# A two-layer conditioned block on one core: the first loads and the down weight's quantisation take other places in layer 0's opening steps

## The chip, the cores and the metric

The kernel runs on one NeuronCore of a Trainium2 chip. The metric is the device time of one launch in microseconds (us), as the median of several runs; a lower time is better. The trace shown below is one profiled execution of the same program. Engine names: PE is TensorE (matmuls; PEld its weight loads), DVE is VectorE, ACT is ScalarE, POOL is GpSimd, SP is SyncE, which here only issues transfers. "SPq" and "ACTq" are instructions that issue a transfer (DMA) from that engine's queue.

## What is computed

Eight sequences of 512 tokens with model width 256 go through two layers, both steered by a vector `cond` per sequence. Layer 0 is a gated feed-forward with a quantised second matmul; layer 1 is adaptive-norm attention with 16 heads, then adaptive-norm SwiGLU. Layer 0, where the change lies, is:

```python
scale = cond @ norm_w.T + 1.0
h = x * (scale[:, None, :] * rsqrt(mean(x * x, -1) + EPS))
val, gate = split(h @ up_w.T, 2, axis=-1)              # up_w: 2048 x 256
h = val * gelu(gate)
s = 127 / clip(max|h| over a row);  hq = clip(round(h * s), -128, 127) / s
t = 1 / clip(mean|down_w|);         wq = clip(round(down_w * t), -1, 1) / t
x1 = hq @ wq.T + x                                     # down_w: 256 x 1024
```

## The kernel before, in words

Layer 0 runs as 32 tiles of 128 tokens. Every engine has its own instruction queue, written out by `phase1_program`: for each step n it first puts what `before_<engine>(n)` gives, then the tile's work `<engine>_tile(n)`. An engine works its queue strictly in this order, and a semaphore wait in it holds all that stands behind. Step n loads and scales tile n, does the up matmuls, the gate and the quantisation of tile n-1 (`UP = 1`), and the down matmul of tile n-3 (`DOWN = 3`). In what follows, m is the number of a tile.

One step, by engine. SP loads `xk` (the tile transposed) and `xt` (its tokens in rows), and issues the transposing transfer `qT <- h_q`. ACT makes `xs` = scaled `xk` (needs `par`, the layer's scale vector), the sum of squares of `xt`, and two gelu halves. DVE copies `xs` to its rounded part (`x_high`, line 412), makes `ms` (415), multiplies gate half 0 (`gate(0)`, 422), then gate half 1 (`gate(1)`), takes the row maximum (452), scales (462) and ends with `h_q` (474). POOL makes the remainder part of `xs` (348, signals `x_split`) and the powers. PE does 12 matmuls of 512 columns for half 0 (gate bank, value bank), then the down matmul of tile n-3 (393), then 12 more for half 1. The matmuls in fp32r are done in three products of high and low parts, so a weight needs its high part (an ACT copy) and its low part (a DVE subtraction).

Weights in the opening. `load_up_sp` (step 1 of SP) loads the up weight in four pieces of 512 columns (512 KB each). `up_high_act` (step 1 of ACT, line 510) makes a piece's high part, `up_low_dve` (step 1 of DVE, line 633) its low part; PE's tile 0 waits for `up_low` piece by piece. `load_small_act` (step 0 of ACT) issues four transfers: `cond`, the layer-0 scale vector's weight (64 KB), the other six vectors' weights (384 KB) and `out_b`. The last two are needed from step 4 of PE and step 5 of DVE on.

The down weight (1 MB) is loaded by SP in step 2 (`load_down_sp`). DVE sums its absolute values in step 1, between `gate(0)` and `gate(1)` (`down_sum_dve`, line 638). In step 2, PE sums that over partitions (`mean_pe`, after its first 12 matmuls); DVE, again between `gate(0)` and `gate(1)`, makes the mean and its reciprocal (`down_mean_dve`), and then three passes over 128 x 2048 elements (`down_quantised_dve`, lines 653, 656, 659), the last of which brings the semaphore `down_steps` to 6. PE's first down matmul, in step 3 between its two groups of 12, waits for it:

```python
if live(n, DOWN):
    m = n - DOWN
    pe.wait_ge(q_turned[m % 2], (m // 2 + 1) * 16)
    if m == 0:
        pe.wait_ge(down_steps, 6)
```

After layer 0, layer 1's attention of one sequence and the feed-forward of the sequence before run together.

Of the kernel before, what the change touches and what calls it, by code (L numbers as in the profile page):

```python
# [5 lines left out]
def cond_seq_kernel(nc, x_tok, xT, condT, vec_wT, up_wT, down_wT, wqT, wkT, wvT, woT, gate_wT, hidden_wT,  # L6
# [40 lines left out]
    with ctx:  # L47
# [359 lines left out]
        def dve_tile(dve, n):  # L407
            if live(n, 0):
                dve.wait_ge(x_scaled, credited(x_scaled, n + 1))
                if n >= 2:  # L410
                    dve.wait_ge(up_val_done, 2 * n - 2)
                nc.vector.tensor_copy(xs_part[0][:, n % 2, :, :], xs[:]).then_inc(x_high, 1)
                dve.wait_ge(square_done, n + 1)
                dve.wait_ge(rstd_done, credited(rstd_done, n))
                nc.vector.tensor_scalar(ms[:], ss[:], 1.0 / D, EPS, ALU.mult, ALU.add).then_inc(ms_done, 1)  # L415

            def gate(j):

                m = n - UP
                dve.wait_ge(up_val_done, 2 * m + j + 1)  # L420
                dve.wait_ge(gelu_done, credited(gelu_done, 2 * m + j + 1))
                nc.vector.scalar_tensor_tensor(h[:, j * W:(j + 1) * W], val_bank[j][:],  # L422
                                               rstd[:, m % 2:m % 2 + 1], gelu[:, j, :], ALU.mult, ALU.mult) \
                    .then_inc(h_done, 1)
            if live(n, UP):
                gate(0)
            if n == 1:
                down_sum_dve(dve)
            if n == 2:
                down_mean_dve(dve)  # L430
                down_quantised_dve(dve)
            if live(n, DOWN):
                m = n - DOWN
                nc.vector.tensor_tensor(dequant[:, m % 2:m % 2 + 1], clipped[:, m % 4:m % 4 + 1], wdeq[:], ALU.mult) \
                    .then_inc(dequant_done, 1)
                dve.wait_ge(dequant_done, m + 1)
                dve.wait_ge(down_done, credited(down_done, m + 1))
                if m >= T:
                    dve.wait_ge(x1_stored[m % T], credited(x1_stored[m % T], m // T * 16))
                nc.vector.scalar_tensor_tensor(x1t[:, m % T, :], down_bank[:, 0:D], dequant[:, m % 2:m % 2 + 1],  # L440
                                               xt[:, m % (T + 1), :], ALU.mult, ALU.add).then_inc(x1_done, 1)
            if live(n, NORM):
                m = n - NORM
                dve.wait_ge(square2_done, m + 1)
                dve.wait_ge(rstd2_done, credited(rstd2_done, m))
                nc.vector.tensor_scalar(ms2[:], ss2[:], 1.0 / D, EPS, ALU.mult, ALU.add).then_inc(ms2_done, 1)
            if live(n, UP):
                m = n - UP
                gate(1)

                dve.wait_ge(h_done, credited(h_done, 2 * m + 2))
                nc.vector.tensor_reduce(amax[:, 0:1], h[:], AX.X, ALU.max, apply_absolute_value=True) \  # L452
                    .then_inc(scale_steps, 1)
                dve.wait_ge(scale_steps, 4 * m + 1)
                nc.vector.tensor_scalar(clipped[:, m % 4:m % 4 + 1], amax[:, 0:1], 1e-5, None, ALU.max) \
                    .then_inc(scale_steps, 1)
                dve.wait_ge(scale_steps, 4 * m + 2)
                nc.vector.reciprocal(amax[:, 1:2], clipped[:, m % 4:m % 4 + 1]).then_inc(scale_steps, 1)
                dve.wait_ge(scale_steps, 4 * m + 3)
                nc.vector.tensor_scalar(amax[:, 2:3], amax[:, 1:2], QMAX, None, ALU.mult).then_inc(scale_steps, 1)  # L460
                dve.wait_ge(scale_steps, 4 * m + 4)
                nc.vector.tensor_scalar(h_rounded[:], h[:], amax[:, 2:3], ROUND, ALU.mult, ALU.add) \
                    .then_inc(rounded, 1)
            if live(n, NORM):
                m = n - NORM
                dve.wait_ge(rstd2_done, credited(rstd2_done, m + 1))
                dve.wait_ge(xn_transposed, credited(xn_transposed, m))
                nc.vector.tensor_scalar(xn[:], x1t[:, m % T, :], rstd2[:], None, ALU.mult).then_inc(xn_done, 1)
            if live(n, UP):
                m = n - UP  # L470
                dve.wait_ge(rounded, m + 1)
                if m >= 2:
                    dve.wait_ge(q_turned[m % 2], m // 2 * 16)
                nc.vector.tensor_scalar(h_q[:, m % 2, :], h_rounded[:], ROUND, QMAX, ALU.subtract, ALU.min) \
                    .then_inc(quantised, 1)

        def load_up_sp(sp):
            src = up_wT.rearrange("(k p) n -> p k n", p=P)
            for i, cols in enumerate(CHUNKS):
                sp.dma_start(up_st[:, :, cols], src[:, :, cols]).then_inc(up_loaded[i], 16)  # L480

        def load_down_sp(sp):
# [19 lines left out]
        def load_small_act(act):  # L502
            act.dma_start(cond_sb[:], condT).then_inc(scale_loaded, 16)
            act.dma_start(vec_w[:, 0, :], vec_wT[:, 0, :]).then_inc(scale_loaded, 16)
            act.dma_start(vec_w[:, 1:7, :], vec_wT[:, 1:7, :]).then_inc(small_loaded, 16)
            act.dma_start(outb_sb[:], out_b.partition_broadcast(B)).then_inc(small_loaded, 16)

# [128 lines left out]
        def down_sum_dve(dve):  # L636
            dve.wait_ge(down_loaded, 16)
            nc.vector.tensor_reduce(absum[:], down_st[:], AX.XY, ALU.add, apply_absolute_value=True) \
                .then_inc(down_steps, 1)
# [7 lines left out]
            nc.vector.reciprocal(wscale[:], mean[:]).then_inc(down_steps, 1)  # L647
            dve.wait_ge(wdeq_ready, 1)

        def down_quantised_dve(dve):  # L650

            dve.wait_ge(down_steps, 3)
            nc.vector.tensor_scalar(down_st[:], down_st[:], wscale[:], 1.0, ALU.mult, ALU.min) \
                .then_inc(down_steps, 1)
            dve.wait_ge(down_steps, 4)
            nc.vector.tensor_scalar(down_st[:], down_st[:], -1.0, ROUND, ALU.max, ALU.add) \
                .then_inc(down_steps, 1)
            dve.wait_ge(down_steps, 5)
            nc.vector.tensor_scalar(down_q[:], down_st[:], ROUND, None, ALU.subtract).then_inc(down_steps, 1)

# [11 lines left out]
        def pieces_at(n):  # L672

            return [i for i in range(len(PIECES)) if n == (3 + i if i < 2 else 5 + (i - 2) // 2)]
# [15 lines left out]
        STACK_SP = [(0, half, r) for half in range(2) for r in range(ROWS // HD)] + [(1, half, 0) for half in range(2)]  # L690

        def before_sp(sp, n):
            if n == 1:
                load_up_sp(sp)
            elif n == 2:
                load_down_sp(sp)
                load_late_sp(sp, (0, 1, 2, 3))
            elif n == 3:
                sp.wait_ge(up_low, len(CHUNKS))
                load_late_sp(sp, (4, 5))  # L700
            elif n == T + 2:
                sp.wait_ge(down_steps, 6)
                load_late_sp(sp, (6,))
            elif n == 2 * T:
                store_alphas_sp(sp)
            elif n == XA_AT:
                for s in range(2):
                    sp.wait_ge(xa_stored[s], credited(xa_stored[s], 2 * 16))
                load_xa_sp(sp, 0)
            elif n == XA_NEXT_AT:  # L710
                for s in range(2):
                    sp.wait_ge(xa_stored[s], credited(xa_stored[s], 4 * 16))
                sp.wait_ge(q_in_low, credited(q_in_low, 1))
                load_xa_sp(sp, 1)
            elif 0 <= n - STACK_AT < 4:
                sp.wait_ge(stack_ones, 2)
                for w, half, r in STACK_SP[2 * (n - STACK_AT):2 * (n - STACK_AT) + 2]:
                    sp.wait_ge(pair_free[w], credited(pair_free[w], 1))
                    stack_dma(sp, 0, w, half, r)

        def before_act(act, n):
            if n == 0:
                load_small_act(act)
            elif n == 1:
                for i in range(len(CHUNKS)):
                    up_high_act(act, i)
            for i in pieces_at(n):
                late_high_act(act, i)
            if n == SPLIT_AT:
# [51 lines left out]
        def before_dve(dve, n):  # L781
            if n == 0:
                scale_dve(dve)
            elif n == 1:
                for i in range(len(CHUNKS)):
                    up_low_dve(dve, i)
            elif n == STORE:
                vectors_dve(dve)
                alphas_dve(dve)
# [1083 lines left out]
```

## Time and profile before

| | us |
|---|---|
| median of 3 runs (lowest, highest) | 996.54 (996.38, 996.85) |
| the profiled execution's own time | 994.97 |
| span of its instructions | 993.1 |
| PE busy in the span | 965.3 (97%) |
| DVE, ACT, POOL busy | 727.9, 552.2, 271.6 |

All times of rows are counted from the first instruction. A row of the timeline is one instruction, or several alike in a run; in brackets stands how long the engine had been idle before it and what ended that. PE's matmuls are pipelined, so the durations of single ones overlap and a "busy" PE includes its overlap. DMA shares are of the 16 DMA engines of the core, and can exceed 1 a little where packets overlap.

### The profile page before, as it was taken

How to read it: one execution, taken by the hardware profiler on the slowest of the kernel's cores; microseconds unless marked ns; L12 is line 12 of the kernel's file. 1: busy time of each engine (PE TensorE's matmuls, PEld its weight loads, DVE VectorE, ACT ScalarE, POOL GpSimd, SP SyncE). 2: the span in 40 equal slices, each digit the busy share in tenths (PEclk: the TensorE clock that was granted, in tenths of full speed). 3: DMA queues.
4: the chain of work that ended last, by engine and by line, in shares of the span. 5: the costliest groups of instructions: out<-in, count | busy, mean ns of one | idle time of the engine just before them, and what ended most of it. 6: DMA issues, size and time to landing. Idle time of an engine off the chain costs nothing.

```text
span 993.1 us, 15671 instructions
## 1 busy us (share of the span) xinstructions
PE 965.3 (97%) x5411; PEld 603.8 (61%) x5411; DVE 727.9 (73%) x1216; ACT 552.2 (56%) x1160; POOL 271.6 (27%) x260
## 2 busy tenths in 40 slices
PE   5999999999999999999999999999999999999998
PEld 4777777776534555655664565556556655655577
DVE  5888888999577777678777767876776777677343
ACT  5466554554655656466556646554764665466632
POOL 1265422221101132222213222231222133134142
PEclk9999999999999999999999999999999999999999
DMA  9645556343431122133021302301230213020000
GB/s 285 150 121 126 139 129 160 96 120 78 107 91 30 65 80 45 41 100 70 1 87 55 70 13 96 90 15 67 73 71 4 84 44 60 30 90 7 2 27 22
DMA packets 93742, 75.45 MB, mean 76 GB/s; under 512 B 44880, under 2 KB 79768, under 8 KB 93664
## 3 DMA queue, kind: packets, MB, share of 16 engines
q1 hardware_dynamic: 81344, 61.36, 22.8%
q10 hardware_dynamic: 12320, 13.09, 5.4%
q8 instruction: 44, 0.72, 0.3%
q14 instruction: 34, 0.28, 0.1%
HBM read 27.73 MB, written 12.61 MB: 41 GB/s over the span
## 4 chain that ended last, share of the span: by engine, by line
PE 86%; DVE 7%; issue 2%; ACT 2%; DMA 2%; ACTq 1%; SPq 0%; POOL 0%; DVEq 0%; POOLq 0%
PE bank L1247 20%; PE bank L370 13%; PE bank L1002 12%; PE bank L1021 12%; PE bank L1291 9%; PE raw_pair L926 5%; PE bank L851 4%; PE bank L902 2%; PE bank L1084 2%; DVE amax L452 2%; PE bank L393 2%; DVE h L422 1%; PE bank L401 1%; PE bank L1397 1%; DVE rowmax L958 1%
## 5 line engine op out<-in xcount | busy, mean ns | idle before, releaser
L1010 ACT ACTIVATE probs<-bank 128x512 f32<-128x512 f32 x512 | 277.0, 598 | 172.1 <-PE bank L1002 165.9
L958 DVE TENSOR_REDUCE rowmax<-raw_pair 128x2 f32<-128x1024 f32 x224 | 273.7, 1222 | 114.8 <-PE raw_pair L926 114.8
L370 PE MATMUL bank<-up_w,xs_part 128*128 128x512 f32 x768 | 191.9, 403 | 5.4 <-issue 3.6
L1002 PE MATMUL bank<-q_stack,k_stack 50*128 50x512 f32 x512 | 189.4, 449 | 2.3 <-ACT probs L1010 1.7
L370 PEld LDWEIGHTS bank<-up_w,xs_part 128*128 128x128 f32 x768 | 142.2, 190 | 39.9 <-issue 6.6
L926 PE MATMUL raw_pair<-k_stack,q_stack 48*128 48x512 f32 x448 | 157.7, 449 | 0.4 <-DVE rowmax L958 0.3
L1277 POOL TENSOR_TENSOR hid<-scratch,hid 128x512 fp32r<-128x512 f32 x64 | 82.4, 1288 | 195.4 <-ACT hid L1273 195.4
L1021 PE MATMUL bank<-probs,v_ext 128*17 128x512 f32 x1024 | 134.8, 598 | 0.9 <-issue 0.9
L1002 PEld LDWEIGHTS bank<-q_stack,k_stack 50*128 50x128 f32 x512 | 76.9, 185 | 84.0 <-issue 51.1
L1291 PEld LDWEIGHTS bank<-out_w,hid 128*128 128x128 f32 x672 | 81.4, 188 | 30.0 <-issue 30.0
L1291 PE MATMUL bank<-out_w,hid 128*128 128x256 f32 x672 | 92.0, 287 | 0.0
L300 ACT ACTIVATE gelu<-bank,rstd 128x512 f32<-128x512 f32 x64 | 44.0, 688 | 57.4 <-PE bank L370 57.4
L1255 ACT ACTIVATE scratch<-bank 128x512 f32<-128x512 f32 x64 | 38.0, 594 | 59.4 <-PE bank L1247 56.6
L926 PEld LDWEIGHTS raw_pair<-k_stack,q_stack 48*128 48x128 f32 x448 | 63.1, 185 | 6.1 <-issue 4.0
L422 DVE SCALAR_TENSOR_TENSOR h<-bank,rstd,gelu 128x512 f32<-128x512 f32 x64 | 47.7, 746 | 23.2 <-PE bank L370 23.2
L348 POOL TENSOR_TENSOR xs_part<-xs,xs_part 128x256 fp32r<-128x256 f32 x32 | 23.6, 738 | 145.5 <-DVE ms L415 127.0
L1259 DVE SCALAR_TENSOR_TENSOR scratch<-scratch,bank 128x512 f32<-128x512 f32 x64 | 43.4, 678 | 14.3 <-ACT scratch L1255 14.3
L1247 PEld LDWEIGHTS bank<-xf_part,gate_w 128*128 128x128 f32 x192 | 33.6, 188 | 33.0 <-issue 27.2
L1247 PE MATMUL bank<-xf_part,hidden_w 128*128 128x512 f32 x192 | 53.2, 412 | 0.0
L1247 PE MATMUL bank<-xf_part,gate_w 128*128 128x512 f32 x192 | 53.1, 412 | 0.0
L1266 DVE SCALAR_TENSOR_TENSOR scratch<-scratch,bank 128x512 f32<-128x512 f32 x64 | 43.9, 686 | 10.2 <-POOL hid L1277 7.7
L1247 PE MATMUL bank<-xa_part,gate_w 128*128 128x512 f32 x186 | 50.4, 406 | 0.0
(185 smaller groups left out, 1332.3 us busy)
## 6 DMA issues: line engine op xcount, KB each, us to landing
q_stack<-split SPq DMA_DIRECT2D x54, 128.0 KB, 3.0
q_stack<-hid SPq DMA_DIRECT2D x42, 128.0 KB, 2.9
k_stack<-hid SPq DMA_DIRECT2D x42, 128.0 KB, 2.9
xk<-xT SPq DMA_DIRECT2D x32, 128.0 KB, 2.8
xt<-x_tok SPq DMA_DIRECT2D x32, 128.0 KB, 2.6
x_spill<-x1t ACTq DMA_DIRECT2D x32, 128.0 KB, 2.5
xa_spill<-xa ACTq DMA_DIRECT2D x32, 128.0 KB, 2.3
x_in<-xa_spill SPq DMA_DIRECT2D x8, 512.0 KB, 5.2
```

What stands on the lines that cost most here:

```text
L300: nc.scalar.activation(gelu[:, j, :], gate_bank[j][:], ACT.Gelu, scale=rstd[:, m % 2:m % 2 + 1]) \
L370: last = nc.tensor.matmul(bank[j][:], xs_part[a][:, m % 2, k, :], up_w[w][:, k, col + j * W:col + (j + 1) * W], start=(i == 0), stop=(i == ...
L422: nc.vector.scalar_tensor_tensor(h[:, j * W:(j + 1) * W], val_bank[j][:], rstd[:, m % 2:m % 2 + 1], gelu[:, j, :], ALU.mult, ALU.mult) \
L926: mm = nc.tensor.matmul(raw_pair[:, half, :], q_stack[rows, slot, qt * P:(qt + 1) * P], k_stack[rows, slot, :], start=True, stop=True)
L958: nc.vector.reduce_max(rowmax[:, e:e + RAWS + 1:RAWS], raw_pair[:], AX.X).then_inc(raw_read, 1)
L1002: nc.tensor.matmul(score_bank[c % 3][:], k_stack[rows, slot, kt * P:(kt + 1) * P], q_stack[rows, slot, :], start=True, stop=True).then_inc ...
L1010: nc.scalar.activation(probs[:, (kt % 2) * J + j, :], score_bank[c % 3][:], ACT.Exp).then_inc(exp_done, 1)
L1021: last = nc.tensor.matmul(o_bank[32 * j:32 * j + HD + 1, :], v_ext[:, kt, J * g + j, :], probs[:, (kt % 2) * J + j, :], start=(kt == 0), s ...
L1247: last = nc.tensor.matmul(work_bank(n, f, spare)[:], weight[wp][:, k, f * P:(f + 1) * P], xf_of(c)[a][:, k, :], start=(i == 0), stop=(i == 5))
L1266: nc.vector.scalar_tensor_tensor(scratch[1][:], scratch[0][:], 0.5, work_bank(1, f, spare)[:], ALU.mult, ALU.mult) \
L1277: nc.gpsimd.tensor_tensor(hid[1][:, f, :], scratch[1][:], hid[0][:, f, :].bitcast(f32), ALU.subtract) \
L1291: last = nc.tensor.matmul(ab[m][:, (t % HALF) * D:(t % HALF + 1) * D], hid[a][:, f, t * P:(t + 1) * P], out_w[wp][:, f, :], start=(i == 0) ...
```

## The change

The first 512 KB piece of the up weight is loaded by SP in step 0, ahead of `xk` and `xt` of tile 0; the other three stay in step 1. ACT makes that piece's high part in step 0, behind its small loads and ahead of tile 0's scaling. The six other vectors' weights and `out_b` are no longer issued in ACT's step 0 but behind the other three high parts in its step 1. DVE's sum of the down weight moves from between the two gates of step 1 to the place behind the four low parts, ahead of tile 1's `x_high`. The three quantising passes are split: the first stays where all three were, the second goes behind `gate(1)`, the third behind `h_q`, all in step 2.

```diff
@@ dve_tile @@
             if live(n, UP):
                 gate(0)
-            if n == 1:
-                down_sum_dve(dve)
             if n == 2:
                 down_mean_dve(dve)
-                down_quantised_dve(dve)
+                down_scaled_dve(dve)
...
                 gate(1)
+                if n == 2:
+                    down_rounded_dve(dve)
...
                 nc.vector.tensor_scalar(h_q[:, m % 2, :], h_rounded[:], ROUND, QMAX, ALU.subtract, ALU.min) \
                     .then_inc(quantised, 1)
+            if n == 2:
+                down_quantised_dve(dve)
@@ loads @@
-        def load_up_sp(sp):
+        def load_up_sp(sp, pieces):
             src = up_wT.rearrange("(k p) n -> p k n", p=P)
-            for i, cols in enumerate(CHUNKS):
+            for i in pieces:
+                cols = CHUNKS[i]
                 sp.dma_start(up_st[:, :, cols], src[:, :, cols]).then_inc(up_loaded[i], 16)
...
             act.dma_start(vec_w[:, 0, :], vec_wT[:, 0, :]).then_inc(scale_loaded, 16)
+
+        def load_vectors_act(act):
             act.dma_start(vec_w[:, 1:7, :], vec_wT[:, 1:7, :]).then_inc(small_loaded, 16)
             act.dma_start(outb_sb[:], out_b.partition_broadcast(B)).then_inc(small_loaded, 16)
@@ down_quantised_dve is cut in three, before each of its waits @@
-        def down_quantised_dve(dve):
+        def down_scaled_dve(dve):
             dve.wait_ge(down_steps, 3)
             nc.vector.tensor_scalar(down_st[:], down_st[:], wscale[:], 1.0, ALU.mult, ALU.min) \
                 .then_inc(down_steps, 1)
+
+        def down_rounded_dve(dve):
             dve.wait_ge(down_steps, 4)
             nc.vector.tensor_scalar(down_st[:], down_st[:], -1.0, ROUND, ALU.max, ALU.add) \
                 .then_inc(down_steps, 1)
+
+        def down_quantised_dve(dve):
             dve.wait_ge(down_steps, 5)
             nc.vector.tensor_scalar(down_q[:], down_st[:], ROUND, None, ALU.subtract).then_inc(down_steps, 1)
@@ before_sp @@
-            if n == 1:
-                load_up_sp(sp)
+            if n == 0:
+                load_up_sp(sp, (0,))
+            elif n == 1:
+                load_up_sp(sp, (1, 2, 3))
@@ before_act @@
             if n == 0:
                 load_small_act(act)
+                up_high_act(act, 0)
             elif n == 1:
-                for i in range(len(CHUNKS)):
+                for i in range(1, len(CHUNKS)):
                     up_high_act(act, i)
+                load_vectors_act(act)
@@ before_dve @@
             elif n == 1:
                 for i in range(len(CHUNKS)):
                     up_low_dve(dve, i)
+                down_sum_dve(dve)
```

## Rows read from the trace of the kernel before

**Rows 1.** Page, part 1: busy us (share of the span) xinstructions, by engine.
```profile
PE 965.3 (97%) x5411; PEld 603.8 (61%) x5411; DVE 727.9 (73%) x1216; ACT 552.2 (56%) x1160; POOL 271.6 (27%) x260
```

**Rows 2.** Timeline of PE (start us, us, what) in layer 0.
```profile
10.47 7.61 PE L370 MATMUL bank<-up_w,xs_part 128*128 128x512 f32 x24 [3.65 <-issue]
18.45 3.06 PE L370 MATMUL bank<-up_w,xs_part 128*128 128x512 f32 x12 [0.37 <-POOL xs_part L348]
...
25.86 3.06 PE L370 MATMUL bank<-up_w,xs_part 128*128 128x512 f32 x12 [1.33 <-POOL xs_part L348]
30.01 1.03 PE L393 MATMUL bank<-down_q,qT 128*128 128x256 bf16 x8 [1.09 <-issue]
...
54.89 5.82 PE L370 MATMUL bank<-up_w,xs_part 128*128 128x512 f32 x24
```

**Rows 3.** Timeline of DVE, steps 0 to 2: low part, sum, passes, first `h_q`.
```profile
9.14 1.23 DVE L633 TENSOR_TENSOR up_w<-up_st,up_w 128x1024 fp32r<-128x1024 f32 x1 [0.79 <-ACT up_w L510]
...
18.46 2.28 DVE L638 TENSOR_REDUCE absum<-down_st 128x1 f32<-128x2048 f32 x1
20.65 0.74 DVE L422 SCALAR_TENSOR_TENSOR h<-bank,rstd,gelu 128x512 f32<-128x512 f32 x1
...
24.04 0.69 DVE L474 TENSOR_SCALAR h_q<-h_rounded 128x1024 bf16<-128x1024 f32 x1
24.65 0.28 DVE L412 CAST xs_part<-xs 128x256 fp32r<-128x256 f32 x1
24.85 0.15 DVE L415 TENSOR_SCALAR ms<-ss 128x1 f32<-128x1 f32 x1
...
28.68 1.23 DVE L659 TENSOR_SCALAR down_q<-down_st 128x2048 bf16<-128x2048 f32 x1
...
33.23 0.69 DVE L474 TENSOR_SCALAR h_q<-h_rounded 128x1024 bf16<-128x1024 f32 x1
```

**Rows 4.** Timeline of ACT and ACTq, steps 0 to 2.
```profile
2.64 0.74 ACTq L506 DMA_DIRECT2D outb_sb<-out_b  x1
...
7.07 0.69 ACT L317 ACTIVATE xs<-xk,par 128x128 f32<-128x128 f32 x2 [2.29 <-DVE par L613]
8.07 1.04 ACT L510 ACTIVATE up_w<-up_st 128x1024 fp32r<-128x1024 f32 x1
...
14.70 1.28 ACT L300 ACT_TABLE_LOAD   x1
...
22.36 0.70 ACT L317 ACTIVATE xs<-xk,par 128x128 f32<-128x128 f32 x2 [1.51 <-DMA xk<-xT]
23.27 0.19 ACT L322 ACTIVATION_READ_ACCUMULATOR square_junk<-xt 128x1 f32 x1
```

**Rows 5.** Windows: us, busy us by engine, clock, DMA share, GB/s.
```profile
3.00:6.00 3.00, 0.00 (x0) 0.00 (x0) 1.00 0.87 226
6.00:9.00 3.00, 0.00 (x0) 0.00 (x0) 1.00 1.01 211
9.00:12.00 3.00, 1.53 (x4) 1.27 (x5) 1.00 1.03 367
```

**Rows 6.** DMA issues: KB, us from issue to landing (issued 1.66, 6.04, 17.11, 24.76).
```profile
up_st<-up_wT SPq DMA_DIRECT2D x1, 512.0 KB, 6.3
down_st<-down_wT SPq DMA_DIRECT2D x1, 1024.0 KB, 11.3
xk<-xT SPq DMA_DIRECT2D x1, 128.0 KB, 5.2
qT<-h_q SPq DMA_TRANSPOSE x1, 4.2
```

**Rows 7.** Timeline of PE at layer 0's end, and the granted clock of two windows there.
```profile
248.40 0.44 PE L401 MATMUL bank<-ident,xn 128*128 128x128 f32 x2 [2.31 <-DVE xn L468]
...
248.40:249.60 1.20, 0.98 (x4) 0.86 (x5) 1.00 0.00 0
249.60:253.00 3.40, 3.40 (x9) 2.30 (x7) 0.50 0.71 156
```

## The prediction

> **What bounds the kernel now.** I read four views in this order. The page's busy times say that PE works 97% of the span [rows 1], so a change counts only by the time at which PE gets through its queue. The timeline of PE shows where it stands still in the opening: it starts at 10.47, waits 0.37 at 18.45, 1.33 at 25.86 and 1.09 at 30.01 [rows 2]; from then on it is as good as gapless (24 matmuls in 5.82 in the steady step [rows 2]) until layer 0's end. So what the change is worth is one number: by how much PE's first down matmul, now at 30.01, moves, since all that follows on PE hangs on it at a fixed distance. The timeline of DVE says what it waits for: the third pass over the down weight runs 28.68 to 29.91, PE starts 0.10 later [rows 2, 3]; the transposed `qT` had landed at 24.76 + 4.2 = 28.96 [rows 6] and was not last. ACT's timeline and the DMA answers say what feeds DVE.
>
> **Start of PE.** Tile 0's `xs` starts at 7.07, when `par` comes [rows 4]. Piece 0 of the up weight lands at 1.66 + 6.3 = 7.96 now [rows 6]. Issued first and without 384 KB on the other queue it lands much earlier: 512 KB at 226 to 367 GB/s [rows 5] takes 1.4 to 2.3, and `xk` of 128 KB in front of it cannot delay it any more, so I estimate 4.5 to 6. Its high part (1.04 [rows 4]) is then hidden under the wait for `par`, up to a landing at 6.0; beyond that each us costs one. `xk` moved behind it is covered the same way. DVE is free for the low part at 9.14 - 0.79 = 8.35 [rows 3] and no longer waits: 8.4 to 9.6, PE at 9.7, 0.8 earlier. At the start PE runs slowly (24 matmuls in 7.61 against 5.82 [rows 2]), and most of the early start falls in that slow time, so tile 0's 24 end at about 17.5 instead of 18.1. The gain for the end is decided elsewhere.
>
> **Transfers.** The non-vector loads ran at 226 and 211 GB/s from 3 to 9 and at 367 after [rows 5]. These 6 us moved 1.31 MB, which takes 3.6 at 367; without the vectors' 0.39 MB as well, 2.5. So loads issued before the vectors can come 0 to 3.5 earlier; I take 2.8, since both the bytes and what slows them go. The down weight then lands not at 6.04 + 11.3 = 17.3 [rows 6] but at 14.5. The vectors now come behind the fourth high part, which ended at 14.70 [rows 4] and will end at about 12; their two issues (0.74 for one [rows 4], 1.4 for both) and the table load (1.28 [rows 4]) stand ahead of gelu half 0 and tile 1's `xs`, which is done by about 16, a us before DVE can take it. Their bytes hit the down weight's end: 0 to 1.1 (0.39 MB at 367), I take 0.2. Landing 14.7.
>
> The Trainium skill ("DMA: Bandwidth & Descriptors", section "Issuing engines are not separate DMA queues") says that transfers of ACT and SP run on the same 16 engines and interleave. A DMA share of 1.01 at only 211 GB/s [rows 5] fits that; by the rule alone moving bytes back returns nothing to loads behind them, tile 2's `xk` would stay at 22.3, and the shift worked out below would be 0.7 more.
>
> **The sum, moved ahead of tile 1 on DVE.** The low parts end at about 13.4 (8.4 + 4 x 1.23 [rows 3]). Before, the sum found its data there; now DVE waits for the landing, 14.7, and sums until 17.0 (2.28 [rows 3]). Queued behind this new wait are tile 1's `x_high`, so POOL's split and PE's tile 1, and both gates. From `x_high` to PE's start it is 25.86 - 24.65 = 1.21 [rows 2, 3], so PE starts tile 1 at 18.2 (18.45 before): nearly nothing. What is gained is on DVE: `gate(1)` of tile 0 comes at about 18.0 instead of 20.65, and, as far behind it as now (24.65 - 20.65 = 4.0 [rows 3]), tile 2's `x_high` could run at 22.0.
>
> **Step 2 of DVE.** `x_high` needs `xs` of tile 2, and that needs `xk`, which landed at 17.11 + 5.2 = 22.3, with ACT waiting for it [rows 4, 6]. By then all vector bytes have been moved in both kernels; only the slow rate can have been saved. 0 to 1.5 earlier, I take 0.7: `xs` from 21.65, and `ms` of tile 2 as far behind it as the read of the squares allows: 23.27 + 0.19 - 22.36 = 1.1 [rows 4], so 22.8. From `ms` at 24.85 to the end of the last instruction of the step, 33.23 + 0.69 = 33.92 [rows 3], are 9.07 us in which DVE does not rest. The change reorders these instructions and removes none. Before, the third pass stood ahead of `gate(1)`, the maximum and `h_q`; now it is last, behind them. So `down_steps` 6 comes at 22.8 + 9.1 = 31.9 and PE's down matmul at 32.0, against 30.01: **2.0 later**. Bounds: with the down weight at 13.9 and `xk` at 20.5, `ms` at 21.2, down matmul at 30.4, +0.4; with the down weight at 15.6 and `xk` unchanged, `ms` at 23.5, 32.7, +2.7. The first pass stays, the second pushes `h_q` of tile 1 by nothing that anyone waits for: its transposed form is needed a step later.
>
> **PE while it waits.** Tile 2's first half can start at max(22.4 + 1.2, 18.2 + 6.1) = 24.3 and ends at 27.35 (3.06 [rows 2]). PE then stands still until 32.0, 4.65 us. The one long pause in the trace outside the start is 2.31 us at 248.40, and behind it the granted clock fell to 0.50 from 249.60 to 253.00, the lower of the two levels, with PE busy throughout [rows 7]; before the pauses of 1.33 and 1.09 nothing fell. The nearest price: the slow start, 7.61 - 5.82 = 1.8, of which about 0.2 was a wait [rows 2]; so **1.6**. From both sides: 0.9 if part of the slow stretch lies in the pause, 2.9 if PE has to work longer before the clock returns. I take 1.6, as 3.4 us at half speed lose 1.7. After it, nothing gives the time back: `x_high` and `gate(0)` of tile 3 stand ready on DVE, and PE is gapless.
>
> **Sum**: +2.0 + 1.6 = +3.6. On the profiled execution's own 994.97 that is 998.6; the median of the runs is 1.57 above that execution, so **1000.1**.
>
> **Rivals.** (a) *The clock holds* through the pause: +2.0, 998.5. For it: a pause of 2.31 let 1.2 us of fast work pass before the fall [rows 7], so the fall depends on how pause and work lie. Against: the pause is twice as long. (b) *Loads early, clock falls*: +0.4 + 1.6 = +2.0, 998.5. (c) *Not slower*: `xk` of tile 2 and the down weight land so early that DVE's step 2 is set by DVE alone. The point from which it decides is `ms` of tile 2 at 20.8 (20.8 + 9.1 = 29.9, today's end of the third pass). That wants `xk` by 19.7, 2.6 earlier than now, and `gate(1)` of tile 0 at 17.0, when tile 0's matmuls have just ended. At its nearest bound, +0.4, with a clock that holds: 996.9; at 20.8: 996.5. (d) *Loads late*: the vectors' bytes sit on the down weight, +2.7 + 1.6 = +4.3, 1000.8, with a long slow clock 1002.1. (e) *The third pass isn't last for PE*: if `qT` took its place, 28.96 is earlier than any of these, so this changes nothing and gets no chance.
>
> **How the numbers follow.** Forecast 0.42; (a) 0.20; (b) 0.10; (c) 0.08; (d) 0.13; a path that I don't see 0.07. A measurement of this kernel can tell about 0.2% (2.0 us) from no change, so the bound is 998.5, on which (a) and (b) lie: half of each counts as slower. Slower: 0.40 + 0.10 + 0.05 + 0.13, less a little for my misreading of an engine's order, 0.65. Faster has no case of its own but the unseen path: 0.05. The rest, 0.30, is within 0.2%. The range goes from (c), 996.6, to the late loads with a longer slow clock, 1001.9.
>
> **What would show it.** Right: PE's start near 9.7; DVE idle ahead of L638, which starts at 14 to 15.5; `ms` of tile 2 at 21.2 to 23.5; the third pass as the last DVE instruction of step 2, near 31.9; an idle time of over 3 us ahead of the first L393 on PE, and a second stretch with the clock at 0.50 behind it. Wrong: a down matmul before 30.0, or a wait ahead of it that ends on `qT`. The forecast is wrong if the low parts or the gate instructions on DVE start much earlier than the landings allow here, or if PE finds other idle time later that swallows the shift.

## The result and the profile after

The changed kernel is slower: 998.28 us as the median of 20 runs (996.34 to 1003.15) against 995.46 of the kernel before in 20 runs beside it (993.66 to 996.85); the ratio is 1.0031, 95% interval 1.0022 to 1.0040. The profiled execution took 998.17 with a span of 996.4. The forecast was +3.6 us, ratio 1.0036; measured are 2.8 by the medians and 3.1 by the ratio.

PE's timeline of the changed kernel, from the start to the steady step; the columns are start us, us, and in brackets the idle time before:

```profile
10.18 11.17 PE L370 MATMUL bank<-up_w,xs_part 128*128 128x512 f32 x36 [3.26 <-issue]
21.18 0.28 PE L611 MATMUL bank<-absum,ones 128*128 128x1 f32 x2
21.32 5.83 PE L370 MATMUL bank<-up_w,xs_part 128*128 128x512 f32 x24
31.45 1.86 PE L393 MATMUL bank<-down_q,qT 128*128 128x256 bf16 x8 [4.31 <-issue]
32.97 4.42 PE L370 MATMUL bank<-up_w,xs_part 128*128 128x512 f32 x12
37.32 1.95 PE L584 MATMUL raw_pair<-cond_sb,vec_w 64*128 64x8 f32 x16
```

Against [rows 2], the waits of 0.37 and 1.33 are gone: tiles 0, 1 and the first half of tile 2 follow each other without a gap, and PE stands in front of its first down matmul at 27.15 instead of 28.92. There it waits 4.31 instead of 1.09, and starts 1.44 later than before. Behind that wait everything is slow: 8 down matmuls take 1.86 instead of 1.03 and the 12 up matmuls behind them 4.42 instead of 3.02 (the row that starts at 30.80 before), 2.2 us together. The windows of the same kernel say why (us, busy us of PE, PEld, DVE, ACT, POOL, then the granted clock, DMA share, GB/s):

```profile
27.15:29.20 2.05, 0.00 (x0) 0.00 (x0) 1.91 (x5) 1.20 (x4) 0.00 (x0) 0.99 0.62 172
29.20:31.40 2.20, 0.00 (x0) 0.00 (x0) 2.17 (x4) 0.00 (x0) 0.00 (x0) 0.50 0.00 0
31.40:36.00 4.60, 4.54 (x15) 3.53 (x16) 1.52 (x5) 0.08 (x1) 2.48 (x3) 0.50 0.54 118
```

The clock fell to its lower level in the middle of the pause and was still there for the next 4.6 us of PE's work, to 36.0. What PE waited for is the last row of DVE's step 2, which ends at 31.35, 0.10 before PE starts; `qT` had landed at 22.60 + 5.6 = 28.2. DVE's timeline of the changed kernel, where it answers to [rows 3]:

```profile
8.36 1.72 DVE L638 TENSOR_TENSOR up_w<-up_st,up_w 128x1024 fp32r<-128x1024 f32 x1
...
14.92 2.29 DVE L643 TENSOR_REDUCE absum<-down_st 128x1 f32<-128x2048 f32 x1 [1.45 <-DMA down_st<-down_wT]
...
22.48 0.28 DVE L412 CAST xs_part<-xs 128x256 fp32r<-128x256 f32 x1
22.69 0.14 DVE L415 TENSOR_SCALAR ms<-ss 128x1 f32<-128x1 f32 x1
...
23.92 1.28 DVE L658 TENSOR_SCALAR down_st<-down_st,wscale 128x2048 f32<-128x2048 f32 x1
25.13 0.74 DVE L422 SCALAR_TENSOR_TENSOR h<-bank,rstd,gelu 128x512 f32<-128x512 f32 x1
25.79 1.21 DVE L663 TENSOR_SCALAR down_st<-down_st 128x2048 f32<-128x2048 f32 x1
26.92 1.21 DVE L452 TENSOR_REDUCE amax<-h 128x1 f32<-128x1024 f32 x1
...
29.52 0.69 DVE L474 TENSOR_SCALAR h_q<-h_rounded 128x1024 bf16<-128x1024 f32 x1
30.13 1.22 DVE L668 TENSOR_SCALAR down_q<-down_st 128x2048 bf16<-128x2048 f32 x1
```

DVE's step 2 starts 2.2 us earlier than before (`ms` at 22.69 against 24.85), yet the third pass ends 1.44 later, at 31.35, because it is now the last instruction of the step. The loads did what was wanted: ACT's high part of piece 0 starts at 4.98 against 8.07 [rows 4], the down weight is there at 14.92 against 17.3 [rows 6], tile 2's `xk` at 21.5 against 22.3. ACT's timeline of the changed kernel:

```profile
4.98 1.06 ACT L515 ACTIVATE up_w<-up_st 128x1024 fp32r<-128x1024 f32 x1 [1.70 <-DMA up_st<-up_wT]
...
11.16 1.06 ACT L515 ACTIVATE up_w<-up_st 128x1024 fp32r<-128x1024 f32 x1 [0.34 <-DMA up_st<-up_wT]
...
21.53 0.70 ACT L317 ACTIVATE xs<-xk,par 128x128 f32<-128x128 f32 x2 [0.86 <-DMA xk<-xT]
```

### The profile page after: what moved, and what is told of

The parts are those of the page before. It is cut to its first block, busy times and chain, and to the rows that moved or that the text cites. A ratio compares the mean times of both kernels' runs of the same rounds, so it can differ in the third digit from the quotient of the medians.

```text
span 996.4 us, 15671 instructions
## 1 busy us (share of the span) xinstructions
PE 966.0 (97%) x5411; PEld 604.5 (61%) x5411; DVE 727.7 (73%) x1216; ACT 552.9 (55%) x1160; POOL 274.0 (28%) x260
## 3 DMA queue, kind: packets, MB, share of 16 engines
q1 hardware_dynamic: 81344, 61.36, 22.8%
## 4 chain that ended last, share of the span: by engine, by line
PE 86%; DVE 7%; issue 2%; DMA 2%; ACT 2%; ACTq 1%; POOL 0%; DVEq 0%; POOLq 0%
PE bank L1261 20%; PE bank L370 14%; PE bank L1016 12%; PE bank L1035 12%; PE bank L1305 9%; PE raw_pair L940 5%; PE bank L865 4%; PE bank L916 2%; PE bank L1098 2%; DVE amax L452 2%; PE bank L393 2%; DVE h L422 1%; PE bank L1411 1%; DVE rowmax L972 1%; PE bank L401 1%
## 5 line engine op out<-in xcount | busy, mean ns | idle before, releaser
L1077 POOL TENSOR_TENSOR split<-o_sb,split 128x512 fp32r<-128x512 f32 x15 | 19.3, 1287 | 113.7 <-ACT split L1073 113.7
```

## The experiments

Theory: the third pass's place makes PE's first down matmul late, and the long pause takes the clock down; the loads gain. Rivals: the loads' order or DVE's new wait ahead of the sum (1.45 us in the row above) costs; the clock plays no part. Each ratio is to the kernel before, run beside it on the same chip, with its 95% interval.

### One part undone: the passes back between the gates

```diff
                 down_scaled_dve(dve)
+                down_rounded_dve(dve)
+                down_quantised_dve(dve)
...
                 gate(1)
-                if n == 2:
-                    down_rounded_dve(dve)
...
-            if n == 2:
-                down_quantised_dve(dve)
```

> The changed kernel with one part undone: all three passes over the down weight stand again between the gates of step 2; the loads and the sum keep their new places. Theory (the third pass's place costs the time, directly and by the clock): the passes end near 27.7, the transposed qT lands at about 28.2 as in the changed kernel (issued 22.60, 5.6 to landing) and is now the last to come, the first L393 starts near 28.3 instead of 31.45 or 30.01, the wait ahead of it is 1 to 1.3, no slow clock follows; 1.7 us faster than before, ratio 0.998 to 0.9985. Rival (the wait of DVE for the down weight ahead of the sum, 1.45 us in the changed kernel, is what costs): that wait is still there, so this stays slower than before, ratio 1.001 or more.

Measured: ratio 0.9978 (0.9969 to 0.9987), faster than before. PE's timeline of this variant around the down matmul:

```profile
29.98 1.05 PE L393 MATMUL bank<-down_q,qT 128*128 128x256 bf16 x8 [1.67 <-DMA qT<-h_q]
30.79 3.03 PE L370 MATMUL bank<-up_w,xs_part 128*128 128x512 f32 x12
33.75 1.95 PE L582 MATMUL raw_pair<-cond_sb,vec_w 64*128 64x8 f32 x16
35.63 1.03 PE L601 MATMUL raw_pair<-vec_w,cond_sb 64*8 64x256 f32 x4
36.59 4.60 PE L370 MATMUL bank<-up_w,xs_part 128*128 128x512 f32 x12
```

The down matmul now waits for `qT`, as expected, and the rival falls: DVE's wait for the down weight is still in this variant. In this execution `qT` took 7.0 us to land (issued 22.95) and the matmul came at 29.98, later than the 28.3 expected. `qT` isn't the whole miss: tile 2's `xk` came late too, `xs` started at 23.31 (21.53 in the changed kernel, with the same loads), and the third pass ended at 29.51 where 27.7 was expected. The profiled execution was also the slowest of this variant's ten runs, 996.36 against a median of 993.43, so its rows show the order of the waits but not the usual times. One row speaks against a part of the theory: the matmuls at 36.59 took 4.60 instead of the 3.04 of the same row before, so the clock fell although the pause had been short. That is taken up below.

### One part alone: the passes in three places

The kernel before with the passes split as in the change, loads and sum untouched.

> The kernel before with one part of the change alone: the three passes in three places, loads and sum as before. Theory: the third pass becomes the last of a DVE step that ended at 33.92, so the first L393 starts at 34.0, 4.0 later than before; the wait ahead of it is about 5 us and the clock falls to its lower level behind it, another 1.6 to 2.3: +5.6 to +6.3 us, ratio 1.0056 to 1.0063. Rival (the load order and the sum cost the time): this is as fast as before, ratio within 0.001 of 1.

Measured: ratio 1.0047 (1.0034 to 1.0061), the slowest of all. The first L393 starts at 34.06 after a pause of 4.70, with the slow clock behind it (1.87 for the 8 matmuls, 4.24 for the 12 behind them). In the traces both shares are as expected: 4.05 for the place and 0.84 + 1.22 = 2.1 for the clock, and the span is 6.1 longer than before (999.2 against 993.1). The ratio shows 4.7, and its interval reaches the 6.1; neither profiled execution lies at its median (994.97 against 996.32 before, 1001.1 against 1000.23 here). The two ways of taking the passes' share agree: 1.0047 alone, and 1.0031 - 0.9978 = 0.0053 on top of the rest of the change.

### One part alone: the loads, and the sum

> The kernel before with the loads' part of the change alone; sum between the gates of step 1 and the three passes between the gates of step 2, as before. Theory: tile 1's x_high no longer waits for the sum and comes at 15.2, the sum runs 16.1 to 18.4, h_q of tile 0 ends near 22.7, tile 2's ms is near 22.9, the third pass ends near 28.0 and the first L393 starts near 28.3: 1.6 to 1.8 us faster than before, ratio 0.998 to 0.9985, the same as the variant that keeps the moved sum. Rival (the loads' order is what costs): slower than before.

> The kernel before with the sum's move alone: DVE sums the down weight behind the four low parts, ahead of tile 1's x_high; loads and passes as before. The variant with the loads alone (ratio 0.9982) and that with loads and sum (0.9978) could not be told apart, so the theory is that the sum's move gives nothing by itself: DVE waits for the landing at 17.3 and sums until 19.6, tile 1 on PE starts at 20.8 instead of 18.45, h_q of tile 0 ends at about 24.8 (24.73 before), the first L393 starts at 30.0 to 30.3. Ratio 0.9995 to 1.001. Rival (the moved sum takes 2.3 us out of the chain from gate(1) to h_q and so gains): the first L393 at 28.5 or earlier, ratio 0.9985.

Measured: the loads alone 0.9982 (0.9972 to 0.9993), the sum alone 1.0014 (1.0001 to 1.0027). With the loads alone the first L393 started at 28.30, as expected, though it waited for `qT` and not for the third pass, which had ended at 27.81. So the gain of the change's good half is the loads'. With the loads, the moved sum makes no difference that the intervals can show (0.9978 against 0.9982). Without them DVE waits as long for the down weight as in the changed kernel (1.45 in both), but all of it is later, and PE waits 1.75 for tile 1. PE's timeline of the sum alone, against 18.45 and 30.01 in [rows 2]:

```profile
20.26 3.05 PE L370 MATMUL bank<-up_w,xs_part 128*128 128x512 f32 x12 [1.75 <-POOL xs_part L348]
...
29.39 1.03 PE L393 MATMUL bank<-down_q,qT 128*128 128x256 bf16 x8 [0.27 <-issue]
...
35.96 4.59 PE L370 MATMUL bank<-up_w,xs_part 128*128 128x512 f32 x12
```

The first down matmul is even 0.6 earlier than before, so 1.0014 isn't explained by it; in that execution too the 12 matmuls behind the vectors' small ones took 4.59 instead of 3.04. These 1.55, less the 0.62, are 0.9 us, and the span of this execution is 0.8 longer than before (993.9 against 993.1): in the trace the clock's fall is the whole loss.

### Which half of the loads' change: piece 0 first, or the vectors behind

```diff
                 load_small_act(act)
+                load_vectors_act(act)
                 up_high_act(act, 0)
...
                     up_high_act(act, i)
-                load_vectors_act(act)
```

> The variant with the passes back in their old place, but the 384 KB of the vectors' weights and out_b are issued again in ACT's step 0; piece 0 of the up weight stays first. It tells which half of the loads' change brings its gain. Theory (the vectors' bytes, and the slow rate beside them, hold up pieces 1 to 3 and all behind them): piece 0 lands at 5 to 7, but piece 3 lands near 13.5 again and the down weight near 17, DVE's wait ahead of the moved sum grows to 1.5 to 3.5, and most of the gain is gone: ratio 0.9995 to 1.001. Rival (only piece 0's place matters): ratio 0.998, piece 3 near 11.

Measured: ratio 1.0000 (0.9990 to 1.0011); with the vectors behind it was 0.9978. ACT's timeline of this variant, then DVE's:

```profile
5.14 1.06 ACT L513 ACTIVATE up_w<-up_st 128x1024 fp32r<-128x1024 f32 x1 [0.44 <-DMA up_st<-up_wT]
...
12.80 1.06 ACT L513 ACTIVATE up_w<-up_st 128x1024 fp32r<-128x1024 f32 x1 [0.34 <-DMA up_st<-up_wT]
```

```profile
16.56 2.29 DVE L641 TENSOR_REDUCE absum<-down_st 128x1 f32<-128x2048 f32 x1 [1.45 <-DMA down_st<-down_wT]
```

Piece 0 comes nearly as early as in the changed kernel (5.14 against 4.98); the fourth piece comes at 12.80 against 11.16, the down weight at 16.56 against 14.92. So most of the gain comes from 392 KB leaving the others' way. What piece 0's place is worth by itself these runs can't tell: 1.0000 stands against 1.0014 of the sum alone, which differs by that place only, and the intervals overlap.

### The clock by itself: work in the pause

```diff
                 m = n - DOWN
+                if m == 0:
+                    for i in range(16):
+                        nc.tensor.matmul(psum[6][:], up_w[0][:, i % KD, 0:P], up_w[0][:, 0, 0:W],
+                                         start=(i == 0), stop=(i == 16 - 1))
                 pe.wait_ge(q_turned[m % 2], (m // 2 + 1) * 16)
```

> The changed kernel with 16 more matmuls of 512 columns into a bank that is free then, ahead of PE's wait for the first down matmul: about 3.7 us of work that nobody needs, in a pause of 4.3. Theory (a part of the loss is TensorE's clock, which fell in that pause and cost 2.1 us at the lower level): the first L393 starts at 31.5 as in the changed kernel, the granted clock stays at its upper level behind it, and the whole is 1.6 to 2.1 us faster than the changed kernel: ratio to before 1.0008 to 1.0014. Rival (the clock is not what costs, the whole loss is the later down weight and what it delays): same time as the changed kernel, ratio 1.003.

Measured: ratio 1.0013 (1.0005 to 1.0022) against 1.0031 of the changed kernel. More work on PE, at the same place of the first down matmul, and 1.8 us less time, give or take 1.2 by the two intervals: only the clock behind the pause is left as its cause. PE's timeline:

```profile
26.86 3.79 PE L390 MATMUL raw_pair<-up_w 128*128 128x512 f32 x16
31.54 1.03 PE L397 MATMUL bank<-down_q,qT 128*128 128x256 bf16 x8 [0.89 <-issue]
32.33 3.03 PE L370 MATMUL bank<-up_w,xs_part 128*128 128x512 f32 x12
...
38.13 4.61 PE L370 MATMUL bank<-up_w,xs_part 128*128 128x512 f32 x12
```

Right behind the pause the clock stayed up (1.03 and 3.03 instead of 1.86 and 4.42, 2.2 us less). But again it fell behind the 20 small matmuls, with no pause over 0.9 us near, and this second fall took 1.6 back (4.61 instead of 3.04). So the two profiled executions differ by only 0.5 in all (998.17 against 997.69). The 1.8 of the runs is what filling the pause gave in sum; what the fall in the pause cost by itself is read from the rows, 2.2.

### How far forward the third pass has to go

```diff
                 if n == 2:
                     down_rounded_dve(dve)
+                    down_quantised_dve(dve)
...
-            if n == 2:
-                down_quantised_dve(dve)
```

> The changed kernel with the third pass moved forward past five instructions only: it stands directly behind the second pass, ahead of the row maximum, and no longer behind h_q. Theory (the distance between the third pass and the front of DVE's step 2 is what PE's first down matmul pays, and only this place costs): DVE still does gate(1) ahead of it, so down_steps 6 comes at about 28.1, 0.4 to 0.7 later than with all passes in their old place, and qT lands at 28 to 30 and is the last; the first L393 at 28.2 to 30, no pause over 3 us, ratio to before 0.998 as for the variant with the passes back (0.9978). Rival (splitting the passes costs by itself, or h_q of tile 1 coming later costs): ratio 1.000 or more.

Measured: ratio 0.9985 (0.9976 to 0.9994); the third pass ran 28.19 to 29.42, `qT` landed at about 29.3 (22.53 + 6.8) and the first L393 started at 29.51, so both came at about the same time. The pass was expected to end at 28.1; it came later since `xs` of tile 2 started only at 22.68 here and `ms` at 23.81. The change would have been a gain with its passes split, had the third not gone behind `h_q`. 0.9985 and 0.9978 lie in each other's intervals.

### The pause used: the vectors' matmuls put into it

```diff
-            elif n == 4:
-                vectors_pe(pe)
...
                 m = n - DOWN
+                if m == 0:
+                    vectors_pe(pe)
                 pe.wait_ge(q_turned[m % 2], (m // 2 + 1) * 16)
```

Once on the changed kernel as it is, once on the variant with the passes back:

> The changed kernel as it is, with PE's 20 small matmuls for the vectors (2.9 us) moved from step 4 into its pause of 4.3 us ahead of the first down matmul. Theory (the loss is that pause and the slow clock behind it, nothing else): the first L393 stays at 31.5, the pause shrinks to 1.4, step 4 is 2.9 shorter, so 2.9 less than the changed kernel's 1.0031, ratio 1.0002; if the small 8-column matmuls do not keep the clock up, the slow stretch stays and it is this; if they do, 1 to 2 us less again, 0.9985. Rival (something on DVE behind the pause is the bound by then): the small matmuls only change places, ratio 1.002 or more.

> The variant with the passes back in their old place, and PE's 20 small matmuls for the vectors (2.9 us, 33.75 to 36.66) moved from step 4 into the pause ahead of the first down matmul. Theory: the pause of 1.6 is filled, the first L393 starts when the small matmuls end, near 29.9, and step 4 is 2.9 shorter; net the length of the pause is gained, 1.6 us: ratio to before 0.9958 to 0.9967. The clock may still fall, as it did at 36.56 in that variant behind these same 8-column matmuls. Rival (the vectors' weights, now loaded late, are not there yet, or the small matmuls delay more than the pause gave): no gain, ratio 0.9978 or more.

Measured: 0.9998 (0.9989 to 1.0006) on the changed kernel, 0.9962 (0.9950 to 0.9975) on the other. In the first, PE has 2.9 us of needed work in its pause, the down matmul stays at 31.9, and 3.3 us (give or take 1.2) are gained against 1.0031, about the 2.9 moved: the pause is real lost time of PE and nothing behind it on DVE takes over. The clock fell all the same, and it did so while the small matmuls ran, ahead of the 1.25 of idle time that was left, so they don't hold it. The window with this fall:

```profile
29.20:30.30 1.10, 1.10 (x6) 0.35 (x5) 1.06 (x2) 0.13 (x2) 0.00 (x0) 0.80 0.00 0
```

PE's timeline of the first, then of the second:

```profile
27.42 1.95 PE L586 MATMUL raw_pair<-cond_sb,vec_w 64*128 64x8 f32 x16
29.30 1.37 PE L605 MATMUL raw_pair<-vec_w,cond_sb 64*8 64x256 f32 x4
31.92 1.86 PE L395 MATMUL bank<-down_q,qT 128*128 128x256 bf16 x8 [1.25 <-issue]
```

```profile
26.88 1.95 PE L584 MATMUL raw_pair<-cond_sb,vec_w 64*128 64x8 f32 x16
28.76 1.03 PE L603 MATMUL raw_pair<-vec_w,cond_sb 64*8 64x256 f32 x4
29.72 1.05 PE L395 MATMUL bank<-down_q,qT 128*128 128x256 bf16 x8
30.52 5.82 PE L370 MATMUL bank<-up_w,xs_part 128*128 128x512 f32 x24
```

The second is the fastest kernel of this study: 991.48 us against 995.33 of the kernel before beside it. PE has no gap from 18.10 to layer 0's steady step.

### Two that gave nothing

SP's loads of the hidden and out weights moved from step 3 to step 4 (`n == 3` becomes `n == 4`), on the variant with the passes back:

> The variant with the passes back in their old place, and SP's loads of the hidden and out weights (2 MB) moved from its step 3 to its step 4, behind the first transposing transfer. In that variant PE's first down matmul waited for qT, which took 7.0 us to land behind those loads (3.0 to 3.1 in a quiet queue). Theory: qT lands 3.1 to 4.5 after its issue, near 26.5, the third pass (27.8 to 29.5) is the last to come, the first L393 starts 0.3 to 1.5 us earlier: ratio to before 0.9965 to 0.9977. Rival (the transfer is slow for another reason, or the next qT, now behind the 2 MB, is late in turn): same time or slower than that variant, ratio 0.998 or more.

Measured: 0.9980 (0.9970 to 0.9991), no gain over 0.9978. In the profiled execution `qT` landed 3.2 us after its issue and the first L393 started at 27.82, as expected and 2.2 before the 29.98 of the other's profiled execution. But the 2.2 set the fastest of this variant's 12 runs (992.15) against the slowest of the other's ten (996.36), and not like against like. A nearer match is the variant with the loads alone, 28.30 with a `qT` of 5.7 us, and there the difference is 0.5. So less than 1 us may have been to be had, which these intervals can't tell; this is argued, not shown.

Seven matmuls on a tile of ones ahead of tile 0, on the fastest variant:

> The fastest variant so far (passes back, small matmuls in the pause, ratio 0.9962) with 7 matmuls of a constant tile of ones (128 columns in fp32, about 0.43 us each at the slow clock) on PE between the scale vector's matmuls and tile 0, where PE stands still from 7.1 to 10.4. Theory: PE's opening runs at the lower clock level because PE did nothing ahead of it; with work ahead, tile 0's 24 matmuls take 5.8 to 6.5 instead of 7.3 and end 0.8 to 1.4 earlier. But tile 1's start waits for DVE, whose moved sum ends at 17.1 and so sets x_high: PE would wait there for what it has gained, gate(1) and h_q come up to 0.9 earlier, and PE's queue, gapless from tile 1 on in that variant, starts at the same 18.1: ratio 0.9955 to 0.9962, no gain that can be told. Rival (PE's own work is the bound from tile 0 on): ratio 0.9948 to 0.9954.

Measured: 0.9966 (0.9953 to 0.9978), no gain, as expected, but not for the reason given: the work did not make tile 0 faster. PE's timeline:

```profile
7.08 3.35 PE L772 MATMUL raw_pair<-ones 128*128 128x128 f32 x14
10.41 7.13 PE L370 MATMUL bank<-up_w,xs_part 128*128 128x512 f32 x24
17.78 3.06 PE L370 MATMUL bank<-up_w,xs_part 128*128 128x512 f32 x12 [0.24 <-POOL xs_part L348]
```

Tile 0's 24 matmuls took 7.13, against 7.26 without that work; 5.8 to 6.5 were expected.

## Why the prediction was right, point by point

**The bound.** Right: one number, the start of the first down matmul, carries the result. It moved by 31.45 - 30.01 = 1.44, and the slow matmuls behind it are the rest; a fixed mark further on, the 24 matmuls that start at 54.89 in the kernel before [rows 2], start at 58.47 in the changed one, 3.58 later, and the whole span is 3.3 longer.

**Start of PE.** Forecast 9.7, measured 10.18. The landing of piece 0 (4.94) was within the estimate. The mis-sized term is the first low part: 1.72 instead of the 1.23 of [rows 3] (see the last section). It cost nothing. PE went from tile 0 to tile 1 without a gap, and on DVE `gate(1)` waited 0.34 for PE at 18.48, and `h_q` ended at 22.57; but the squares that `ms` needs were read only at 22.63 (22.44 + 0.19 on ACT), so `ms` could not have come sooner.

**Transfers.** Down weight 14.9 (forecast 14.7), `xk` of tile 2 21.5 (21.6). Without the vectors among them, all loads together ran at 307 and 323 GB/s from 3 to 9 instead of 226 and 211 [rows 5]; these two rates of before are of all loads too, not of "the non-vector loads" as the forecast has it, and its sum takes them so. The Trainium skill ("DMA: Bandwidth & Descriptors", section "Issuing engines are not separate DMA queues") says that transfers of all issuing engines interleave on the same 16 DMA engines; the forecast's reading of that alone would have left `xk` at 22.3, and in this execution it came 0.8 sooner. So bytes moved back did not cost later what they had cost in front. The place of `xk` isn't a fixed one, though: with the same loads `xs` of tile 2 started between 20.85 and 21.86 in seven profiled executions, and at 22.68 and 23.31 in two. The runs with the vectors in front (1.0000) and behind (0.9978) show the difference as time. The windows of the changed kernel:

```profile
3.00:6.00 3.00, 0.00 (x0) 0.00 (x0) 1.00 0.95 307
6.00:9.00 3.00, 0.00 (x0) 0.00 (x0) 1.00 0.97 323
```

**The sum ahead of tile 1.** Forecast: wait to 14.7, end at 17.0, tile 2's `x_high` possible at 22.0. Measured 14.92, 17.2, and 22.48. The forecast's lowest bound, +0.4, has a slip here: with `xk` at 20.5 its own 1.1 from `xs` to `ms` gives `ms` at 21.65 and not 21.2, so +0.8.

**Step 2 of DVE.** `ms` at 22.69 (22.8). From there to the end of the step I took 9.07 from before; it took 8.66 (22.69 to 31.35). That is the mis-sized term of the first price, 0.4 of the 0.56 by which 2.0 was too much. The rows show where: the passes used to follow each other, each starting 1.26 to 1.33 after the one whose result it takes; now the gate starts 1.21 behind the first, the second pass 0.66 behind the gate, the maximum 1.13 behind the second. The instructions that don't need their neighbour's result start 0.07 to 0.08 before that has ended.

**The clock.** Forecast 1.6, bounds 0.9 to 2.9. In the profiled execution 3.58 - 1.44 = 2.1; filling the pause gave 1.8 over many runs (1.0031 - 1.0013). The 1.6 came from the opening, where PE is slow but the granted clock reads 1.00 [rows 5], so that row does not show a price of the clock; the forecast's other basis does, 3.4 us at half speed. What it had too short is the stretch: 6.8 us (29.2 to 36.0), of which 4.6 were PE's work. Rival (a), the clock holds, is out as a description of this kernel; the variant in which it holds behind the pause came to 1.0013, below the 2.0 us forecast for it, since the first price was smaller. Rivals (b), (c) and (d) didn't come: the landings lay between their bounds.

**The sum.** 1.44 + 2.1 = 3.6 in the profiled execution, by chance the forecast's 3.6 from 2.0 + 1.6; both errors were about half a us and of opposite sign. (The ends of the forecast's range, 996.6 and 1001.9, also aren't quite its rivals' own numbers, 996.5 or 996.9 and 1002.1; the result doesn't turn on it.) The execution's own time rose by 3.2 (998.17 - 994.97) and the medians by 2.8. By where the two profiled executions lie among the runs this closes: that of before is 0.5 under its median, that of after 0.1 under its own. Within the traces the 3.58 at 54.89 have become 3.46 at layer 0's end (248.40 against 251.86) and 3.31 behind it. Before, the clock fell there [rows 7]; in the changed kernel's profile, behind the same pause of 2.31, it stayed at 1.00. That was worth 0.15 and not the 1.4 that the matmuls took less, since PE then waited 1.26 for a `qT` for which it had not waited before. The row of before, then the windows and the row of the changed kernel:

```profile
253.02 1.06 PE L393 MATMUL bank<-down_q,qT 128*128 128x256 bf16 x8
...
250.00:254.00 4.00, 2.14 (x11) 1.80 (x12) 3.83 (x10) 1.02 (x3) 0.00 (x0) 1.00 0.09 19
254.00:258.00 4.00, 2.74 (x18) 2.07 (x17) 1.73 (x7) 1.22 (x4) 0.55 (x1) 1.00 0.52 115
...
256.33 0.94 PE L393 MATMUL bank<-down_q,qT 128*128 128x256 bf16 x7 [1.26 <-DMA qT<-h_q]
```

The forecast priced a slow stretch for the new pause and did not reckon with the old one, which need not come in each execution. The absolute 1000.1 also stood on a median of before from 3 runs, 996.54, which was 1.1 above that of 20. Against the forecast's own bound for "slower", 998.5, the median of 998.28 would have fallen just short; it is slower by the runs of before beside it, whose interval is narrower than the 0.2% assumed.

## What to carry to other kernels

Where an engine works its queue in order and another waits for its result, a chain of instructions that is scattered between other work is late by everything that now stands ahead of its last one; reckon the one that signals, not the sum of the chain. Gains made upstream (here 2.2 us on DVE) are lost if the last link moves back further than that. And a pause on TensorE is a place for its own small work from later: moved into it, 2.9 us of matmuls cost nothing here.

## What the runs showed of the hardware that was not expected

**A pause doesn't have to be long, or be there at all, for the clock to fall.** In four variants with pauses of at most 1.7 us nearby, the 12 up matmuls behind the vectors' 20 small ones took 4.59 to 4.61 instead of 3.05. The windows of the variant with the passes back, PE busy throughout:

```profile
33.75:36.60 2.85, 2.85 (x22) 2.14 (x21) 2.78 (x6) 0.51 (x2) 2.47 (x3) 0.99 0.57 106
36.60:40.00 3.40, 3.40 (x9) 2.72 (x9) 2.36 (x6) 0.45 (x1) 0.00 (x0) 0.50 0.31 106
```

The one thing they have in common is what PE did ahead: 16 matmuls with 8 columns and 4 with 256, 2.9 us in which PE counts as busy in the profile. It is not enough by itself: in the kernel before, with the loads alone, with the third pass ahead of the maximum, with SP's loads in step 4, and in the fastest variant, where it fills the pause, the same stretch left the clock up. The pause of 2.31 at layer 0's end is alike: of the 13 profiled executions the clock fell behind it in 4 and stayed up in 9, among these all 7 in which it had fallen in the opening. What decides is open. That executions of one kernel differ is shown by the mean granted clock of each run: of 78 runs of the kernel before, taken beside the variants, 17 had 1.000 and took 994.8 us on average, and 61 had 0.997 to 0.999 and took 995.9.

**The slow opening differs between executions of like kernels.** Tile 0's 24 matmuls took 7.61 before, 8.43 with the passes back, 8.59 with the sum alone and 7.26 in the fastest, all with the same operands; work on a tile of ones ahead of them changed nothing (7.13). In the kernel before and with the sum alone 0.6 and 0.7 of it can be the wait for a low part. The granted clock reads 1.00 throughout (9 to 12 before, [rows 5]), so that the profile doesn't show this slowness as the lower level, and its cause stays open.

**DVE and POOL were slow side by side.** In the changed kernel the first low part on DVE took 1.72 (the other three 1.21), and POOL's power beside it 1.54 instead of the 0.57 of the one at 18.19. POOL's power took as long again, 1.62, where the first pass over the down weight ran beside it; that pass itself was not slower (1.28). POOL's timeline of the changed kernel:

```profile
8.27 0.73 POOL L348 TENSOR_TENSOR xs_part<-xs,xs_part 128x256 fp32r<-128x256 f32 x1 [3.87 <-DVE xs_part L412]
8.95 1.54 POOL L353 TENSOR_TENSOR rstd<-ms,minus_half 128x1 f32<-128x1 f32 x1
...
23.62 1.62 POOL L353 TENSOR_TENSOR rstd<-ms,minus_half 128x1 f32<-128x1 f32 x1
```

The slow powers end when DVE's instruction has ended or soon after: 10.49 against 10.08, and 25.24 against 25.20. Overlap alone doesn't do it. Before, the low part started at 9.14, when about half of that power (8.86 to 9.42) had run, and both kept their times (1.23 [rows 3] and 0.56); but POOL's split of `xs` had ended at 8.90 there, while in the changed kernel it ran beside the low part. And in the variant with the passes alone the first pass started 0.32 us behind the power (26.52 against 26.20), which took 0.55. No run was made for this alone, so that one holds up the other is argued, not shown.
